# Normalised values, joint value products and a two-term spread in a pipelined four-stage attention kernel

## The chip, the cores and the metric

One core of one Trainium2 chip runs the whole program. The metric is the device time of one execution in microseconds (us), the median of three runs. TensorE (PE in the rows) multiplies, VectorE (DVE), ScalarE (ACT) and GpSimd (POOL) do the elementwise work, SyncE (SP) issues the transfers.

## The reference

Sixty-four images, 256 channels of 14 x 14, go through four blocks in turn:

```python
x = _L0_conv_ref(x, ...)  # batchnorm, depthwise 3x3 + 1x1 for q, k, v; k and v resized to 7x7; 4 heads, softmax; depthwise + 1x1, MLP
x = _L1_conv_ref(x, ...)  # group norm (8 groups); linear attention: softmax(k) over channels, softmax(q) over tokens
x = _L2_conv_ref(x, ...)  # group norm (32 groups); 8-head softmax attention over 196 tokens; projection; residual
x = _L3_conv_ref(x, ...)  # group norm (32 groups); single-head attention over 196 tokens; projection; residual
```

Each group norm is `(x - mean) * rsqrt(var + eps)`, then a weight and a bias for each channel. Everything is float32.

## The kernel before

Two images (a pair) are one unit of work: 32 pairs, 392 columns each, channels in two chunks of 128 partitions. The four blocks are cut into named steps (`q0_0`, `kv1`, `gn3`, `sc2`, `t3_1` and so on). The program is a software pipeline: each engine has a table from step to a place (`PE_AT`, `ACT_AT`, `DVE_AT`, `POOL_AT`, `SP_AT`). A place divided by `SLOTS` = 128 gives the lag, by how many turns of the loop the step comes after its pair entered; the remainder gives its place in the turn. So an engine's order in one turn is that of the remainders, over steps of up to six different pairs. A place is no time: engines work in order and wait for semaphores alone. `BANK_USES` says which PSUM bank (a, b, c, e; `ps_s` has four of its own) holds the result of a TensorE step; a bank must be read out before the next step of the turn writes it.

Names that follow in the text, in the order in which a pair meets them:
- `k0`, `v0`: keys and values of block 0 from the resized convolution output `yr`, which GpSimd makes (`resize0`, `resize1`). `pw`, `mlp`: its last products.
- `stats1..3` on VectorE, `gn1..3` on TensorE (a product with a group matrix) and on VectorE (a copy out of PSUM), then `gn1..3` on GpSimd: `normalized` makes scale and shift of each channel in 20 small instructions of 128x4 (a square root by Newton steps), and then applies them with four instructions of 128x196 (`xn`). `high` (ScalarE, to float32r) and `low` (VectorE, the rest) split the normalised values in two terms for products in float32r. These feed `kv0..3`, `q1` (block 1), `hq`, `hk`, `hv` (block 2), `v3_0..3`, `q3` (block 3).
- `keys0..3`: the exponentials of block 1's keys times the reciprocal of their sum, on GpSimd. `ctx`, `out`: the products behind them.
- `sc0..3` scores of block 2 (four heads at a time), `max` on VectorE, exponentials `sc` on ScalarE, `tn` transposes and their copies, `av` products. `rden`, `rt`: reciprocals of the sums, turned. `rep0`, `rep1`: the reciprocals spread over the channels by a product with the 0/1 matrix `heads`, `proj` behind them.
- `s3`, `probs3_0`, `probs3_1` (probabilities of block 3 times the reciprocal, on GpSimd), `t3`, `o3`.

Of the kernel before, what the change touches and what calls it, by code (L numbers as in the profile page):

```python
# [22 lines left out]
R7 = 7  # L23
# [15 lines left out]
    "x": -128, "res": 204, "hop": 486, "hop_out": 665, "store": 691,  # L39
# [38 lines left out]
}  # L78

POOL_AT = {  # L80
    "resize0": 64, "resize1": 73, "probs0": 146, "probs1": 164, "gn1": 301, "keys0": 347, "keys1": 356, "keys2": 365,
    "keys3": 374, "gn2": 393, "gn3": 640, "rows3": 667, "probs3_0": 694, "probs3_1": 722,
}

# [37 lines left out]
def build(nc, a):  # L122
    ctx = ExitStack()
    with ctx:
# [399 lines left out]
        def _(pool):  # L524
# [7 lines left out]
            def alone():  # L532

                pool.sem_inc(pool_held, 1)
# [1013 lines left out]
```

## Time and profile before

| | |
|---|---|
| median of 3 runs | 2321.23 us (2320.8 to 2322.84) |
| the profiled execution | 2331.84 us, its span 2329.6 us |
| mean granted TensorE clock | 0.975 |
| PE busy | 2158.8 us (93%) |
| DVE busy | 1851.9 us (79%) |
| ACT busy | 1443.0 us (62%) |
| POOL busy | 1493.3 us (64%) |

Busy times are unions over an engine's instructions in the one profiled execution. Times of "start to start" in the text are differences of the start column of a timeline, and take in the pipelining that durations do not show.

### The profile page before, as it was taken

The page shows a single profiled execution, that of the slowest core. Times are in us where ns is not written, and L with a number is a line of the kernel's source. Part 1 is how long each engine was busy: PE and PEld are TensorE (multiplying, and loading weights), DVE is VectorE, ACT ScalarE, POOL GpSimd, SP SyncE. Part 2 cuts the span into 40 slices and gives each one's busy share as a digit, 9 for nine tenths or more (in the row PEclk, how much of TensorE's full clock was granted, in tenths as well). Part 3 has the DMA queues.
Part 4 walks back from the last instruction along what each step waited for, and adds up shares of the span by engine and source line. Part 5 has one row for each costly group of instructions (what it writes and reads, how often), then busy time and mean ns, then how long its engine had stood idle before and what let it go on. Part 6 is the DMA issues. An engine that isn't in the chain of part 4 may idle for free. (4 is left out here: it accounts for less than half of the span.)

```text
span 2329.6 us, 59692 instructions
## 1 busy us (share of the span) xinstructions
PE 2158.8 (93%) x15488; PEld 1724.9 (74%) x15488; DVE 1851.9 (79%) x4359; ACT 1443.0 (62%) x4819; POOL 1493.3 (64%) x3274
## 2 busy tenths in 40 slices
PE   5679999999999999999999999999999999999987
PEld 4456777777777777778777777777777777777775
DVE  6678788888888888888888888888888888887542
ACT  2246666666666666666666676666667666666663
POOL 3665667676666767666676766667676666775422
PEclk8699999999999999999999999999999999999997
DMA  3000011000000000000000001000000001000000
GB/s 117 14 22 22 15 36 36 34 21 14 34 34 34 34 34 21 14 34 34 34 34 27 28 14 34 34 34 34 21 34 14 34 34 34 28 29 29 15 29 21
DMA packets 29829, 70.24 MB, mean 30 GB/s; under 512 B 6260, under 2 KB 7104, under 8 KB 29760
## 3 DMA queue, kind: packets, MB, share of 16 engines
q1 hardware_dynamic: 26928, 67.68, 8.3%
q10 hardware_dynamic: 2832, 1.73, 0.3%
q8 instruction: 33, 0.54, 0.1%
q14 instruction: 36, 0.29, 0.0%
HBM read 30.86 MB, written 12.85 MB: 19 GB/s over the span
## 5 line engine op out<-in xcount | busy, mean ns | idle before, releaser
L831 ACT ACTIVATE e<-ps_s,nm 98x196 f32<-98x196 f32 x1024 | 421.5, 431 | 80.6 <-DVE nm L955 80.6
L1159 DVE SCALAR_TENSOR_TENSOR y<-opad,w_dw,y 128x406 f32<-128x406 f32 x512 | 303.9, 646 | 0.0
L1140 DVE SCALAR_TENSOR_TENSOR y<-xpad,w_dw,y 128x406 f32<-128x406 f32 x512 | 297.9, 644 | 0.0
L955 DVE TENSOR_REDUCE nm<-ps_s 98x4 f32<-98x784 f32 x256 | 244.7, 969 | 54.8 <-PE ps_s L1167 52.3
L590 POOL TENSOR_SCALAR xn<-x,gn_scale,gn_shift 128x196 f32<-128x196 f32 x384 | 264.5, 701 | 21.3 <-POOL gn_shift L585 21.3
L568 POOL TENSOR_TENSOR gn_t<-gn_group 128x4 f32<-128x4 f32 x96 | 29.6, 308 | 325.6 <-DVE gn_group L1005 249.6
L838 ACT COPY pt<-ps_s 98x392 f32<-98x392 f32 x512 | 223.4, 508 | 13.5 <-PE ps_s L1217 13.4
L1093 DVE TENSOR_TENSOR xs<-xn,xs 128x392 fp32r<-128x392 f32 x192 | 133.0, 695 | 108.9 <-ACT xs L788 106.8
L831 ACT ACTIVATION_READ_ACCUMULATOR e<-ps_s,nm 98x1 f32 x1024 | 217.1, 212 | 0.0
L1217 PE MATMUL ps_s<-w_eye,e 98*98 98x98 f32 x2048 | 202.6, 252 | 2.9 <-ACT e L831 2.7
L1217 PEld LDWEIGHTS ps_s<-w_eye,e 98*98 98x98 f32 x2048 | 187.2, 131 | 8.8 <-ACT e L831 4.8
L1167 PE MATMUL ps_c<-ws_v,xs 128*98 128x256 f32 (+1 forms) x960 | 139.1, 292 | 36.6 <-DVE xs L1093 36.6
L788 ACT CAST xs<-xn 128x392 fp32r<-128x392 f32 x192 | 100.1, 525 | 94.7 <-POOL xn L590 88.9
L1167 PEld LDWEIGHTS ps_c<-ws_v,xs 128*98 128x98 f32 x960 | 118.4, 165 | 46.2 <-DVE xs L1093 26.5
L581 POOL TENSOR_SCALAR gn_t<-gn_t 128x4 f32<-128x4 f32 x288 | 115.9, 403 | 56.2 <-POOL gn_t L579 56.2
L611 POOL TENSOR_SCALAR kv<-kv,rk 98x256 f32<-98x256 f32 x128 | 129.2, 1016 | 31.6 <-DVE rk L1023 31.1
L845 ACT COPY a<-ps_s 128x196 f32<-128x196 f32 x128 | 41.7, 326 | 163.7 <-PE ps_s L1167 163.7
L634 POOL TENSOR_SCALAR e<-e,r 98x196 f32<-98x196 f32 x128 | 105.7, 837 | 37.1 <-DVE r L1113 29.6
L755 ACT ACTIVATE kv<-kv,nmk 98x256 f32<-98x256 f32 x128 | 64.7, 507 | 100.4 <-DVE nmk L1017 100.3
L1167 PE MATMUL ps_s<-k,q 32*98 32x196 f32 x2048 | 118.8, 345 | 2.7 <-ACT k L807 1.4
L579 POOL TENSOR_TENSOR gn_t<-gn_t,gn_half 128x4 f32<-128x4 f32 x288 | 104.9, 364 | 22.6
L936 DVE BATCH_NORM_STATS2 gn_stats<-x 128x6 f32<-128x196 f32 x384 | 110.9, 351 | 9.2 <-DVE x L1049 5.3
(235 smaller groups left out, 5820.0 us busy)
## 6 DMA issues: line engine op xcount, KB each, us to landing
x_in<-in_x SPq DMA_DIRECT2D x32, 392.0 KB, 3.1
x_res<-in_x SPq DMA_DIRECT2D x32, 392.0 KB, 3.2
x2b<-x SPq DMA_DIRECT2D x32, 392.0 KB, 3.3
out<-x SPq DMA_DIRECT2D x32, 392.0 KB, 3.3
out_pairs<-out SPq DMA_DIRECT2D x32, 392.0 KB, 2.4
w_q<-in_q SPq DMA_DIRECT2D x3, 256.0 KB
w_k<-in_k SPq DMA_DIRECT2D x3, 256.0 KB
w_v<-in_v SPq DMA_DIRECT2D x3, 256.0 KB
```

The lines of the kernel that those rows point to most:

```text
L581: link(g.tensor_scalar(t.t[:], t.t[:], 1.5, None, ALU.add))
L590: g.tensor_scalar(dst[:, c, of_image(i)], src[:, c, of_image(i)], t.scale[:, j:j + 1], t.shift[:, j:j + 1], ALU.mult, ALU.add).then_inc(t. ...
L611: g.tensor_scalar(kv[:, j, 0:CH], kv[:, j, 0:CH], rk[:, j:j + 1], None, ALU.mult).then_inc(k_scaled.sem, 1)
L831: s.activation(e2[:, j, tc], tile(use)[0:HALF, of_image(tc)], ACT.Exp, bias=nm2[:, j, tc:tc + 1], accum_out=den2[:, 2 * i + tc, h:h + 1]). ...
L838: s.copy(turned(j), tile(use)[0:HALF, 0:N2]).then_inc(emptied(use), 1)
L936: v.bn_stats(t.stats[:, j], src[:, j // 2, of_image(j % 2)]).then_inc(t.stat_steps.sem, 1)
L955: v.tensor_reduce(out=nm2[:, two], in_=ps_s[0:HALF, two, 0:N2].rearrange("p b (c n) -> p b c n", c=2), axis=AX.X, op=ALU.max, negate=True) ...
L1093: v.tensor_tensor(dst[:, 1, c], src[:, c], dst[:, 0, c], ALU.subtract).then_inc(gn[n].low.sem, 1)
L1140: v.scalar_tensor_tensor(out=dst, in0=window(xpad, c, k, CR), scalar=tap, in1=dst, op0=ALU.mult, op1=ALU.add).then_inc(conv1_steps.sem, 1)
L1159: v.scalar_tensor_tensor(out=dst, in0=window(opad, c, k, CR), scalar=tap, in1=dst, op0=ALU.mult, op1=ALU.add).then_inc(conv2_steps.sem, 1)
L1167: return nc.tensor.matmul(dst, lhsT, rhs, start=start, stop=stop)
L1217: last = nc.tensor.transpose(tile(use)[0:HALF, of_tile(sc, tc)], e2[:, j, tc, sc * HALF:(sc + 1) * HALF], eye[0:HALF, 0:HALF])
```

## The change

1. `v0`: the two images' values come from one product over 128 columns of weights (both images side by side in `yr`), not from one product for each image over a doubled copy of `yr`. The resize on GpSimd no longer writes the doubled copy. ScalarE takes the result out in four copies instead of two.
2. `rep0`, `rep1`: the reciprocals `rt2` are kept as two float32r terms (ScalarE makes the first, VectorE the rest), `heads` as float32r, and the spread is two float32r products of 392 columns for each `rep`, not two float32 products of 196.
3. `normalized` becomes `coefficients`: GpSimd makes scale and shift alone. Applying them (`norm1..3`), the scaling of the keys (`keys0..3`) and of block 3's probabilities (`probs3_0`, `probs3_1`) go to ScalarE.
4. All five tables and `BANK_USES` are made anew (one line of them stands below).

```diff
 POOL_AT = {
-    "resize0": 64, "resize1": 73, "probs0": 146, "probs1": 164, "gn1": 301, "keys0": 347, "keys1": 356, "keys2": 365,
-    "keys3": 374, "gn2": 393, "gn3": 640, "rows3": 667, "probs3_0": 694, "probs3_1": 722,
+    "resize0": 128, "resize1": 144, "probs0": 208, "probs1": 240, "gn1": 352, "gn2": 432, "gn3": 672, "rows3": 704,
...
-                link(g.tensor_copy(yr[:, c, :, 1, 0:T7], yr[:, c, :, 0, 0:T7]))
...
-                for c in range(KC):
-                    for i in range(2):
-                        j = 2 * c + i
-                        alone()
-                        g.tensor_scalar(dst[:, c, of_image(i)], src[:, c, of_image(i)], t.scale[:, j:j + 1],
-                                        t.shift[:, j:j + 1], ALU.mult, ALU.add).then_inc(t.done.sem, 1)
...
+                        p = pair_of(t, u, ACT_AT[f"keys{j}"])
+                        if p is not None:
+                            act.wait_ge(k_rsum.sem, k_rsum.at(p, j + 1))
+                            s.activation(kv[:, j, 0:CH], kv[:, j, 0:CH], ACT.Copy, scale=rk[:, j:j + 1]).then_inc(k_scaled.sem, 1)
...
+                    for n, src, dst in ((1, x1, xn1), (2, x2, xn2), (3, x3, xn3)):
+                        for c in range(KC):
+                            p = pair_of(t, u, ACT_AT[f"norm{n}_{c}"])
+                            if p is not None:
+                                act.wait_ge(gn[n].steps.sem, gn[n].steps.at(p + 1, 0))
...
+                                    s.activation(dst[:, c, of_image(i)], src[:, c, of_image(i)], ACT.Identity,
+                                                 scale=gn[n].scale[:, j:j + 1], bias=gn[n].shift[:, j:j + 1]
+                                                 ).then_inc(gn[n].done.sem, 1)
...
+                            for j in (2 * i, 2 * i + 1):
+                                s.activation(e3[:, j], e3[:, j], ACT.Copy, scale=r3[:, j:j + 1]).then_inc(p3_done.sem, 1)
...
-                        v.tensor_copy(rt2[:], tile("rt")[0:H2, 0:N2]).then_inc(emptied("rt"), 1)
+                        v.tensor_tensor(rt2[:, 1], tile("rt")[0:H2, 0:N2], rt2[:, 0], ALU.subtract).then_inc(emptied("rt"), 1)
...
-                        for i in range(2):
-                            last = product(tile("v0")[:, i * CH:(i + 1) * CH],
-                                           lambda k: yr[:, k, i].rearrange("p a n -> p (a n)"), lambda k: w["v0"][:, k])
+                        product(tile("v0")[:, 0:CH], lambda k: yr[:, k].rearrange("p i n -> p (i n)"),
+                                lambda k: w["v0"][:, k]).then_inc(filled("v0"), 1)
...
-                            for c in range(KC):
-                                last = mm(tile(use)[:, of_image(c)], w["heads"][:, c], rt2[:, of_image(i)], True, True)
+                            product(tile(use)[:, 0:N2], lambda k: heads[:, c], lambda k: rt2[:, k]).then_inc(filled(use), 1)
```

Where the instructions stand, at the three places that matter below. TensorE from `hq0` to `sc0`, before (the third row is `v0`, the fourth `gn1`):

```order
L1167 MATMUL ps_c<-xs2,ws_q2 128x392 x6
...
L1167 MATMUL ps_b<-xs2,ws_k2 128x392 x6
...
L1167 MATMUL ps_e<-w_v0,yr 128x256 x4
...
L1167 MATMUL ps_a<-gn1_mine,w_group32 128x8
...
L1167 MATMUL ps_s<-k2,q2 98x196 x8
```

and after:

```order
L1173 MATMUL ps_c<-xs2,ws_q2 128x392 x6
...
L1173 MATMUL ps_a<-xs2,ws_k2 128x392 x6
...
L1173 MATMUL ps_b<-gn1_mine,w_group32 128x8
...
L1173 MATMUL ps_c<-w_v0,yr 128x256 x2
...
L1173 MATMUL ps_s<-k2,q2 98x196 x8
```

`v0` has two products instead of four and has moved behind `gn1`; a `rep` row reads `ps_b<-rt2,w_heads 128x196 x2` before and `ps_c<-rt2,heads 128x392 x2` after, four products a pair in both, in float32r after.

ScalarE at the end of a turn, from the second `ctx` copy to the split of block 3's input, before (`xs3` is the `high` step, `q0` and `pt2` copies out of PSUM, `e2` the exponentials of `sc2`):

```order
L778 ACTIVATE cx<-ps_c,rq 128x256 x2
...
L831 ACTIVATE e2,den2<-ps_s,nm2 98x196 x2
...
L788 CAST xs3<-xn3 128x392
...
L701 COPY q0<-ps_e 128x392
...
L788 CAST xs3<-xn3 128x392
L831 ACTIVATE e2,den2<-ps_s,nm2 98x196 x2
...
L831 ACTIVATE e2,den2<-ps_s,nm2 98x196 x4
```

and after:

```order
L758 ACTIVATE cx<-ps_e,rq 128x256 x2
...
L834 ACTIVATE e2,den2<-ps_s,nm2 98x196 x6
...
L774 ACTIVATE xn3<-x3,gn3_shift,gn3_scale 128x196 x2
...
L676 COPY q0<-ps_c 128x392
L774 ACTIVATE xn3<-x3,gn3_shift,gn3_scale 128x196 x2
L841 COPY pt2<-ps_s 98x392
...
L785 CAST xs3<-xn3 128x392
```

The turn ends there; the next one begins with three more `COPY pt2` and then the second `CAST xs3`. Two pairs of normalisations now stand ahead of the casts, and the exponentials of `sc2` ahead of both.

ScalarE around block 2's split, before (`qt3` is the `q3` copy, `s0` an exponential of block 0):

```order
L838 COPY pt2<-ps_s 98x392
...
L788 CAST xs2<-xn2 128x392
...
L788 CAST xs2<-xn2 128x392
...
L862 ACTIVATE qt3<-ps_c,qu3 128x392
L725 ACTIVATE s0<-s0 98x392
```

and after:

```order
L857 COPY v3t<-ps_c 98x257
L841 COPY pt2<-ps_s 98x392
...
L774 ACTIVATE xn2<-x2,gn2_shift,gn2_scale 128x196 x4
...
L785 CAST xs2<-xn2 128x392
...
L785 CAST xs2<-xn2 128x392
...
L841 COPY pt2<-ps_s 98x392 x3
```

The four normalising instructions stand straight ahead of the two casts, and three `pt2` copies have moved behind them.

## Rows read from the trace of the kernel before

**Rows 1.** Windows: length, then busy us of PE, PEld, DVE, ACT, POOL, clock, DMA.

```profile
1201.00:1269.06 68.06, 65.60 (x484) 52.59 (x482) 57.81 (x136) 44.78 (x150) 46.96 (x103) 1.00 0.08 29
267.50:2106.70 1839.20, 1772.05 (x13012) 1420.34 (x13011) 1553.69 (x3640) 1207.79 (x4048) 1271.20 (x2757) 1.00 0.08 29
```

**Rows 2.** Waits of TensorE, 267.5 to 2106.7: total us, times, longest.

```profile
PE ps_b L1459 <- POOL e L634: 35.8, 27, 1.4
PE ps_c L1167 <- DVE xs L1093: 21.8, 26, 1.2
PE ps_b L1167 <- DVE xs L1093: 9.0, 27, 0.5
```

**Rows 3.** Timeline of TensorE, one turn: start, us, tiles, idle before.

```profile
1201.00 1.48 PE L1167 MATMUL ps_e<-y,w_q 128*128 128x392 f32 x4
...
1205.98 0.96 PE L1167 MATMUL ps_c<-ws_v,xs 128*98 128x258 f32 x6 [0.80 <-DVE xs L1093]
1206.77 1.59 PE L1217 MATMUL ps_s<-w_eye,e 98*98 98x98 f32 x16
1208.15 0.96 PE L1167 MATMUL ps_b<-ws_v,xs 128*98 128x258 f32 x6
1208.95 1.48 PE L1167 MATMUL ps_a<-y,w_o 128*128 128x392 f32 x4
...
1211.21 0.31 PE L1167 MATMUL ps_e<-gn_mine,w_group 128*128 128x8 f32 x2
...
1212.25 1.58 PE L1167 MATMUL ps_e<-y,w_o 128*128 128x392 f32 x4
...
1224.11 0.87 PE L1167 MATMUL ps_s<-pt,v 98*32 98x196 f32 x16
1224.91 1.33 PE L1167 MATMUL ps_c<-xs,ws_q 128*128 128x392 f32 x6
1226.09 1.23 PE L1167 MATMUL ps_b<-xs,ws_k 128*128 128x392 f32 x6
1227.16 1.89 PE L1167 MATMUL ps_e<-w_v,yr 128*128 128x256 f32 x8
1228.88 0.28 PE L1167 MATMUL ps_a<-gn_mine,w_group 128*128 128x8 f32 x2
...
1234.18 0.93 PE L1167 MATMUL ps_b<-rt,w_heads 8*128 8x196 f32 x4
1235.04 0.56 PE L1295 MATMUL ps_a<-w_eye,p 98*128 98x98 f32 x4
```

**Rows 4.** Timeline of GpSimd: first and last coefficient instruction, block 2, block 3.

```profile
1211.97 0.39 POOL L568 TENSOR_TENSOR gn_t<-gn_group 128x4 f32<-128x4 f32 x1 [7.20 <-DVE gn_group L1005]
...
1220.47 0.20 POOL L585 TENSOR_TENSOR gn_shift<-w_gn_b,gn_t 128x4 f32<-128x4 f32 x1
...
1259.82 0.38 POOL L568 TENSOR_TENSOR gn_t<-gn_group 128x4 f32<-128x4 f32 x1
...
1267.76 2.89 POOL L585 TENSOR_TENSOR gn_shift<-w_gn_b,gn_t 128x4 f32<-128x4 f32 x1
```

**Rows 5.** Groups by shape, whole span: busy us, mean ns | idle before.

```profile
L831 ACT ACTIVATE e<-ps_s,nm 98x196 f32<-98x196 f32 x1024 | 421.5, 431 | 80.6 <-DVE nm L955 80.6
L748 ACT ACTIVATE act<-x,bn_shift,bn_scale 128x392 f32<-128x392 f32 x64 | 45.7, 714 | 13.0 <-DVE x L986 11.9
L778 ACT ACTIVATE cx<-ps_c,rq 128x256 f32<-128x256 f32 x64 | 26.9, 471 | 57.2 <-PE ps_c L1167 57.2
L788 ACT CAST xs<-xn 128x392 fp32r<-128x392 f32 x192 | 100.1, 525 | 94.7 <-POOL xn L590 88.9 <-PE ps_a L1402 3.4
L1093 DVE TENSOR_TENSOR xs<-xn,xs 128x392 fp32r<-128x392 f32 x192 | 133.0, 695 | 108.9 <-ACT xs L788 106.8
```

**Rows 6.** Timeline of ScalarE: an exponential and the next of its kind.

```profile
1249.28 0.43 ACT L831 ACTIVATE e<-ps_s,nm 98x196 f32<-98x196 f32 x1
...
1249.68 0.43 ACT L831 ACTIVATE e<-ps_s,nm 98x196 f32<-98x196 f32 x1
```

More of the change, by code:

```diff
@@ L457, in build @@
         FOLDED = KC * 4
-        EARLY_STEPS = PLAIN + FOLDED + 6
+        EARLY_STEPS = PLAIN + FOLDED + 7
         @block.sync
@@ L604, in step @@
                                             ALU.mult).then_inc(l0_probs.sem, 1)
-                    for j in range(4):
-                        p = pair_of(t, u, POOL_AT[f"keys{j}"])
-                        if p is not None:
-                            pool.wait_ge(k_rsum.sem, k_rsum.at(p, j + 1))
-                            alone()
-                            g.tensor_scalar(kv[:, j, 0:CH], kv[:, j, 0:CH], rk[:, j:j + 1], None, ALU.mult).then_inc(k_scaled.sem, 1)
                     p = pair_of(t, u, POOL_AT["rows3"])
@@ L676, in split_weights @@
                     s.copy(high, src).then_inc(early_high, 1)
+                s.copy(heads[:], w["heads"][:]).then_inc(early_steps, 1)
                 act.wait_ge(early_steps, EARLY_STEPS)
@@ L716, in step @@
                             act.wait_ge(*full(p - 1, latest("o0_0", "o0_1")))
-                        src = tile("v0")[:].rearrange("p (i m d) -> p i m d", i=2, m=2)
-                        for hl in range(2):
-                            half = slice(64 * hl, 64 * hl + 64)
-                            s.copy(v0[half, :, :, half], src[half, :, :, half]).then_inc(emptied("v0"), 1)
+                        src = tile("v0")[:, 0:CH].rearrange("p (m d) -> p m d", m=2)
+                        for i in range(2):
+                            for hl in range(2):
+                                half = slice(64 * hl, 64 * hl + 64)
+                                s.copy(v0[half, i, :, half], src[64 * i:64 * i + 64, :, half]).then_inc(emptied("v0"), 1)
                     for i in range(2):
@@ L779, in step @@
                                              scale=rq[:, c, i:i + 1]).then_inc(emptied(use), 1)
+                    for n, src, dst in ((1, x1, xn1), (2, x2, xn2), (3, x3, xn3)):
[3 more added lines that the diff above has]
+                                act.wait_ge(gn[n].steps.sem, gn[n].steps.at(p + 1, 0))
+                                if n == 1 and has_before(p):
+                                    act.wait_ge(*read(p - 1, f"out{c}"))
+                                if n == 2:
+                                    act.wait_ge(gn[2].low.sem, gn[2].low.at(p, 0))
+                                if n == 3 and has_before(p):
+                                    act.wait_ge(*full(p - 1, latest("s3_0", "s3_1")))
+                                for i in range(2):
+                                    j = 2 * c + i
+                                    s.activation(dst[:, c, of_image(i)], src[:, c, of_image(i)], ACT.Identity,
+                                                 scale=gn[n].scale[:, j:j + 1], bias=gn[n].shift[:, j:j + 1]
+                                                 ).then_inc(gn[n].done.sem, 1)
                     for n, src, dst, readers in splits:
@@ L817, in step @@
                             s.copy(v2[:, i].rearrange("p c n -> p (c n)"), tile(use)[0:HALF, :]).then_inc(emptied(use), 1)
+                    p = pair_of(t, u, ACT_AT["rt"])
+                    if p is not None:
+                        act.wait_ge(*full(p, "rt"))
+                        if has_before(p) and not comes_after("rt", latest("rep0", "rep1")):
+                            act.wait_ge(*full(p - 1, latest("rep0", "rep1")))
+                        s.copy(rt2[:, 0], tile("rt")[0:H2, 0:N2]).then_inc(rt_high.sem, 1)
                     for g in range(GROUPS):
@@ L843, in step @@
                             if has_before(p):
-                                act.wait_ge(*read(p - 1, f"rep{i}"))
+                                act.wait_ge(*read(p - 1, f"rep{g % 2}"))
                             s.copy(a2[:, i, g % 2], tile(use)[:, 0:TOK]).then_inc(emptied(use), 1)
@@ L1060, in step @@
                     if p is not None:
-                        dve.wait_ge(*full(p, "rt"))
-                        if has_before(p) and not comes_after("rt", latest("rep0", "rep1")):
-                            dve.wait_ge(*full(p - 1, latest("rep0", "rep1")))
-                        v.tensor_copy(rt2[:], tile("rt")[0:H2, 0:N2]).then_inc(emptied("rt"), 1)
-                    for i in range(2):
-                        use = f"rep{i}"
+                        dve.wait_ge(rt_high.sem, rt_high.at(p, 1))
+                        v.tensor_tensor(rt2[:, 1], tile("rt")[0:H2, 0:N2], rt2[:, 0], ALU.subtract).then_inc(emptied("rt"), 1)
+                    for c in range(KC):
+                        use = f"rep{c}"
                         p = pair_of(t, u, DVE_AT[use])
@@ L1404, in step @@
                         last.then_inc(filled("rt"), 1)
-                    for i in range(2):
-                        use = f"rep{i}"
+                    for c in range(KC):
+                        use = f"rep{c}"
                         p = pair_of(t, u, PE_AT[use])
```

67 lines of the change are left out of this document (28 added, 39 removed), and 60 rows, old and new, of tables (ACT_AT, DVE_AT, PE_AT).

## The prediction

> **What bounds the kernel now.** I read the windows first. In one turn of the loop (the work of one pair on every engine) TensorE is busy 65.60 of 68.06 us, VectorE 57.8, GpSimd 47.0, ScalarE 44.8, at a granted clock of 1.00, the higher of its two levels (2.4 GHz) [rows 1]. So TensorE is the bound. The stretch from 267.5 to 2106.7 holds 27 turns of 1839.2 / 27 = 68.1 us; the rest of the span is filling and draining. Next I read TensorE's waits in that stretch. There are three, each once a turn [rows 2]: before the transposes `t3_1`, for the probabilities from GpSimd, 35.8 / 27 = 1.3 us; before `v3_1`, for the split of block 3's input, 0.8; before `kv0`, for block 1's, 0.3. Together 2.5 us, and 65.6 + 2.5 = 68.1: the turn is explained. All three end on a chain through GpSimd: the first names it, and the other two are group norms whose coefficients and normalisation it makes. Then I read the timelines of TensorE and GpSimd around these waits.
>
> **The change part by part.**
> *Values of block 0.* `v0` takes 1228.88 - 1227.16 = 1.72 us start to start for eight instructions (each float32 product is two) [rows 3]. Half of the products go, the width of each is the same: -0.86 us a turn.
> *The spread.* A `rep` takes 1235.04 - 1234.18 = 0.86 us for four instructions [rows 3]. It becomes two float32r products of 392 columns. The nearest row is `hq0`, six float32r products of 392 columns in 1226.09 - 1224.91 = 1.18 us, 0.197 each [rows 3]: 0.39 instead of 0.86, twice, -0.94 us. Bounds: nothing saved (0.86 stays, if eight rows of weights cost more than I think), or 0.94. I take 0.94, since the column count is what the other rows follow. TensorE's work falls to 65.6 - 0.86 - 0.94 = 63.8 us.
> *The three waits.* The probabilities, keys and normalisations leave GpSimd. `t3_1` now waits for two ScalarE instructions that stand some 8 us of TensorE work ahead of it in the new order, so the 1.3 us goes. The other two chains keep the coefficients on GpSimd, and the question is what is late next.
> *ScalarE's new work.* An application of scale and bias to 128x196 is not in the trace. Below it lies the exponential of 196 columns, 0.43 us long and 0.40 from start to start, read-out of its sum included [rows 5, 6]; above it the relu of twice the columns with both operands, 0.71 [rows 5]. I take 0.46 a step: it has the relu's operands and the exponential's length. Twelve make 5.5 us. Keys and probabilities: eight, by the `ctx` copy with a scale, 0.47 long, 0.42 a step [rows 5]: 3.4. Two more copies for `v0` and one for `rt`: 0.9. ScalarE goes from 44.8 to 54.6 us of some 65, VectorE stays at 57.8 (its `rt` changes from a copy to a subtraction of the same 392 columns), GpSimd drops well below both. None is the bound by its sum; the order must decide.
> *Block 3's chain, at the turn's end.* In the new order ScalarE has, between the end of the second `ctx` product and `v3_1`: the `ctx` copies 0.84, six exponentials 2.4, four normalisations 1.84, and seven copies or casts of 392 columns (0.525 long, 0.43 a step [rows 5]) 3.0, together 8.1. Then `low` on VectorE, 0.6 to 0.7 [rows 5], and handing over, some 0.4: 9.1. TensorE does in that time `q0_1`, both `out`, `tn2`, `k0`, `pw0`, `gn2` and `av2`, all of which stand before between 1201.00 and 1212.25 [rows 3], with two `v3` products (0.79 and 0.80) and the wait of 0.8 among them: 11.25 - 0.79 - 0.80 - 0.81 = 8.85. The wait left is 0.3 us, from 0 to 1.3 (if a normalisation takes 0.71).
> *Block 2's chain.* From `gn2` to `hq0` the trace has 1224.91 - 1211.21 = 13.7 us without a wait [rows 3]; the new order puts `v3_1` and `v3_0` in and takes one `av` (1224.91 - 1224.11 = 0.80) out: 14.5 us of cover. The chain: 0.76 to the first coefficient instruction, 8.7 for twenty of them (1211.97 to 1220.67) [rows 3, 4], four normalisations 1.84, two casts 0.86, `low` 0.65, handing over 0.5: 13.3. Spare 1.2 us. But block 3's twenty took 1259.82 to 1270.65, 10.8 us, with one of them at 2.89 instead of 0.20 [rows 4]; at that pace block 2's chain is 15.4, and `hq0` waits 0.9.
> *Block 1's chain* has 34.5 - 16.6 = 17.9 us of TensorE work over it in the new order, by the same laying end to end, against 13.3 to 15.4: no wait.
> *Transfers.* The five on SP's queue have moved in the turn. No engine's wait in the stretch names one [rows 2], and each is asked for more than 5 us before its reader: nothing.
> I take 1.0 us of waits a turn: 0.3, half of 0.9, and 0.3 for banks read out late by a fuller ScalarE. The turn is 64.8 us, 3.3 less. Over 27 turns -89, and -1 in the draining turns. Against the profiled span: 2329.6 - 90 = 2239.6. The profiled execution is 2.2 us longer than its span, and 10.6 longer than the median, so the median falls to 2321.2 - 90 = 2231.
>
> **The rivals.**
> *A, no wait is left.* The turn is TensorE's 63.8: 27 x 4.3 = 116, 2205 us. For it: GpSimd, the source of all three waits, is nearly idle. Against: the 9.1 over 8.85 above.
> *B, the coefficients, or ScalarE behind them, are the new wait.* The small GpSimd instructions do not always take 0.20 us: 2.89 beside VectorE's depthwise taps [rows 4]. If block 2's and block 3's chains both lose about one us more than I took, waits are 2 to 2.5 us a turn: 27 x 2.3 = 62 to 27 x 1.8 = 49 less, 2259 to 2272. Against: in block 2's place the same instructions took 8.7.
> The Trainium skill, "GPSIMD Engine Reference", section Key points, says that GpSimd shares its SBUF interfaces with VectorE and is held up by VectorE instructions with two SBUF inputs; the depthwise taps are such, and the 2.89 us row agrees. By that rule the chains stay slow wherever the taps stand beside them, which is B.
> *C, slower: ScalarE in its order becomes the bound.* Elementwise work that waited on its own engine now stands in ScalarE's queue, and every TensorE bank is read out behind it. The turn passes 68.1 us when TensorE waits over 4.3 us. At 0.71 a normalisation the two chains gain 1.0 each and waits come to 3 at most. At 1.2 us each chain gains 3.0, the waits are 7, the turn 70.8: 2394. It decides from about 0.9 us an instruction; the rows stop at 0.71.
> The Trainium skill, "ScalarE: Activation LUTs", Rules for kernel authors, sends plain adds and multiplications to VectorE instead of ScalarE, which speaks for C; the same page's figures for an instruction with two per-partition operands give an estimate near 0.44 us a step, which speaks against it. No run here shows either yet.
> *D, nothing gained:* the float32r spread costs what it did, and the new order brings back 2.5 us of waits with some more in filling: 2300 to 2321.
>
> **How the numbers follow.** My forecast, 2215 to 2248, has 0.60; A 0.12; B 0.20; C 0.04; D 0.04. A measurement of this kernel tells 0.2% (5 us) from no change. Faster is all but C and part of D, 0.94; same 0.02; slower 0.04. The range takes in A's end and B's: 2203 to 2272.
>
> **What would show it.** In the profile after: `v0` four instructions in about 0.86 us, each `rep` two in 0.4; no wait of TensorE on GpSimd; normalisations 0.5 to 0.6 us long; TensorE at 98% or more of a turn; its largest waits before `v3_1` or `hq0`, for VectorE's `low`. The prediction is wrong if ScalarE's normalisations are far longer, if GpSimd's coefficients take over 11 us, or if TensorE waits at steps that I did not lay out, such as those held by a bank.

## The result, and the profile after

The changed kernel takes 2195.69 us (median of 4 runs, 2190.08 to 2196.51) where the kernel before takes 2321.88 beside it (4 runs): ratio 0.9452, 95% interval 0.9435 to 0.9468. It is faster, and by more than the forecast of 2231 us said: the time lies 7 us below the range's lower end, 2203.

| | before | after |
|---|---|---|
| profiled execution, its span | 2331.84, 2329.6 us | 2195.19, 2193.4 us |
| turn, mean of 27 | 68.12 us | 63.62 us |
| from the start to the second `rden` on VectorE (filling) | 267.5 us | 255.7 us |
| behind the 27 turns (draining) | 222.9 us | 220.1 us |
| PE, DVE, ACT, POOL busy, share of the span | 93, 79, 62, 64% | 96, 83, 77, 40% |

The turn is taken from one `rden` to the next here. The windows of the kernel after, one turn and 27 turns (columns as in [rows 1], to which they answer):

```profile
1204.38:1268.00 63.62, 63.53 (x476) 51.70 (x475) 56.98 (x136) 52.44 (x174) 27.34 (x81) 1.00 0.09 32
255.70:1973.30 1717.60, 1715.35 (x12800) 1396.06 (x12799) 1534.07 (x3640) 1414.50 (x4671) 739.16 (x2161) 1.00 0.09 32
```

TensorE is busy 63.53 of 63.62 us. Its list of waits from 255.7 to 1973.3, where [rows 2] had three, is empty; the list leaves out idle gaps under 0.1 us. ScalarE went from 44.8 to 52.4 us a turn, GpSimd from 47.0 to 27.3. Against the forecast for the profiled span, 2239.6, 46 us are missing: 27 x (64.8 - 63.62) = 32 in the turns, 12 in the filling, 2 in the draining.

TensorE in one turn after (compare [rows 3]; third column ahead of the tiles: the modelled length; a step's cost is the difference of two starts):

```profile
1199.24 0.28 PE L1173 MATMUL ps_e<-gn_mine,w_group 128*128 128x8 f32 x2
1199.45 0.88 PE L1173 MATMUL ps_s<-pt,v 98*32 98x196 f32 x16
1200.41 0.96 PE L1173 MATMUL ps_e<-ws_v,xs 128*98 128x258 f32 x6
...
1213.62 1.23 PE L1173 MATMUL ps_c<-xs,ws_q 128*128 128x392 f32 x6
1214.78 0.87 PE L1173 MATMUL ps_s<-pt,v 98*32 98x196 f32 x16
...
1216.89 1.11 PE L1173 MATMUL ps_c<-w_v,yr 128*128 128x256 f32 x4
1217.93 0.92 PE L1173 MATMUL ps_s<-k,q 32*98 32x196 f32 x16
...
1225.81 0.62 PE L1173 MATMUL ps_c<-rt,heads 8*128 8x392 f32 x2
1226.36 1.34 PE L1173 MATMUL ps_b<-xs,ws_k 128*128 128x392 f32 x6
```

`v0` takes 1217.93 - 1216.89 = 1.04 us, a `rep` 1226.36 - 1225.81 = 0.55. `hq0` (1213.62) doesn't wait. `v3_1` (1200.41) does, by an amount below the list's 0.1: `av2` ahead of it takes 0.96 us to the next start, where every other `av` of 16 products takes 0.80 (1224.91 - 1224.11 in [rows 3]), so 0.15 us of each turn is waiting. The elementwise work ahead of the two, on ScalarE and VectorE:

```profile
1191.88 0.84 ACT L758 ACTIVATE cx<-ps_e,rq 128x256 f32<-128x256 f32 x2
...
1199.07 0.59 ACT L785 CAST xs<-xn 128x392 fp32r<-128x392 f32 x1
...
1209.17 1.88 ACT L774 ACTIVATE xn<-x,gn_shift,gn_scale 128x196 f32<-128x196 f32 x4 [0.44 <-POOL gn_shift L587]
```

```profile
1199.66 0.17 DVE L1013 COPY gn_group<-ps_e 128x8 f32<-128x8 f32 x1 [0.74 <-PE ps_e L1173]
1199.79 0.57 DVE L1099 TENSOR_TENSOR xs<-xn,xs 128x392 fp32r<-128x392 f32 x1
...
1211.78 0.57 DVE L1000 TENSOR_TENSOR x<-ps_c,x 128x392 f32<-128x392 f32 x1 [0.74 <-PE ps_c L1173]
1212.27 1.03 DVE L1099 TENSOR_TENSOR xs<-xn,xs 128x392 fp32r<-128x392 f32 x2
```

and block 2's coefficients on GpSimd, the first, the longest and the last of twenty (compare [rows 4]):

```profile
1199.98 0.43 POOL L570 TENSOR_TENSOR gn_t<-gn_group 128x4 f32<-128x4 f32 x1 [12.00 <-DVE gn_group L1013]
...
1204.05 2.01 POOL L581 TENSOR_TENSOR gn_t<-gn_t,gn_half 128x4 f32<-128x4 f32 x1
...
1208.86 0.20 POOL L587 TENSOR_TENSOR gn_shift<-w_gn_b,gn_t 128x4 f32<-128x4 f32 x1
```

Block 3's chain: its `low` ends at 1199.79 + 0.57 = 1200.36, 0.05 ahead of `v3_1`, so it is what `v3_1` waits for. But ScalarE does not set that end. The cast is done at 1199.66; `low` stands in VectorE's order behind the copy of `gn2`, which waits 0.74 for TensorE's own `gn2` product (1199.24). In the kernel of 2188 us further down, whose normalisations are on GpSimd, the second cast ends 0.65 us earlier, counted from the `ctx` product, and `v3_1` comes 8.56 us behind that product as it does here. Its rows, cast, copy and `low`:

```profile
1194.59 0.55 ACT L809 CAST xs<-xn 128x392 fp32r<-128x392 f32 x1
```

```profile
1195.79 0.17 DVE L1032 COPY gn_group<-ps_e 128x8 f32<-128x8 f32 x1 [0.75 <-PE ps_e L1192]
1195.92 0.57 DVE L1118 TENSOR_TENSOR xs<-xn,xs 128x392 fp32r<-128x392 f32 x1
```

In the kernel after, `low` begins 0.13 us behind its cast, where one that only waits for its cast begins 0.03 behind: the slack of ScalarE's part is 0.1.

Block 2's `low` ends at 1213.30, 0.32 ahead of `hq0`; that `low` stands in VectorE's order behind the addition for `mlp1`, which itself waited 0.74 for TensorE, so the chain can be later than the 0.32 tells. Four normalisations take 1.88 us.

The question for the experiments: where the gain of 4.5 us a turn comes from (products, moved work, timetable), and why next to no wait is left.

### The profile page after: what moved, and what is told of

Read it like the earlier page. It is cut to its first block, busy times and chain, and to the rows that moved or that the text cites. A ratio compares the mean times of both kernels' runs of the same rounds, so it can differ in the third digit from the quotient of the medians.

```text
span 2193.4 us, 58372 instructions
## 1 busy us (share of the span) xinstructions
PE 2096.0 (96%) x15232; PEld 1692.7 (77%) x15232; DVE 1830.2 (83%) x4359; ACT 1689.1 (77%) x5556; POOL 887.0 (40%) x2570
## 4 chain that ended last, share of the span: by engine, by line
PE 88%; POOL 3%; DVE 3%; ACT 3%; issue 2%; SPq 1%; DMA 0%; DVEq 0%; POOLq 0%; ACTq 0%
PE ps_b L1173 18%; PE ps_c L1173 18%; PE ps_a L1173 17%; PE ps_e L1173 16%; PE ps_s L1173 9%; PE ps_s L1223 7%; DVE xs L1099 1%; POOL gn_y L584 1%; ACT e L834 1%; ACT xn L774 1%; PE ps_b L1461 1%; PE ps_e L1406 0%; SPq L477 0%; PE ps_b L1299 0%; PE ps_c L1461 0%
## 5 line engine op out<-in xcount | busy, mean ns | idle before, releaser
L774 ACT ACTIVATE xn<-x,gn_shift,gn_scale 128x196 f32<-128x196 f32 x384 | 190.1, 566 | 36.1 <-POOL gn_shift L587 36.1
L1223 PEld LDWEIGHTS ps_s<-w_eye,e 98*98 98x98 f32 x2048 | 186.1, 128 | 29.7 <-ACT e L834 10.8
L1099 DVE TENSOR_TENSOR xs<-xn,xs 128x392 fp32r<-128x392 f32 x192 | 107.3, 586 | 43.7 <-ACT xs L785 43.6
L598 POOL TENSOR_TENSOR p<-s,r 98x392 f32<-98x392 f32 x64 | 56.4, 882 | 194.4 <-DVE r L986 194.4
L581 POOL TENSOR_TENSOR gn_t<-gn_t,gn_half 128x4 f32<-128x4 f32 x288 | 125.9, 437 | 22.5
L1173 PE MATMUL ps_a<-xs,ws_q 128*128 128x392 f32 x576 | 126.7, 355 | 0.0
L1173 PE MATMUL ps_s<-pt,v 98*32 98x196 f32 x2048 | 114.5, 342 | 1.4 <-ACT pt L841 1.3
L1173 PEld LDWEIGHTS ps_s<-k,q 32*98 32x98 f32 x2048 | 76.5, 160 | 38.5 <-issue 29.7
L1173 PE MATMUL ps_c<-y,w_q 128*128 128x392 f32 x256 | 101.0, 518 | 4.0 <-ACT q L676 3.1
L1173 PEld LDWEIGHTS ps_a<-xs,ws_q 128*128 128x128 f32 x576 | 98.2, 189 | 0.1
L549 POOL TENSOR_TENSOR rs_d<-y 128x168 f32<-128x168 f32 x64 | 39.6, 619 | 144.2 <-DVE y L1146 139.6
```

The costliest lines, as they stand in the source:

```text
L581: link(g.tensor_tensor(t.t[:], t.t[:], t.half[:], ALU.mult))
L774: s.activation(dst[:, c, of_image(i)], src[:, c, of_image(i)], ACT.Identity, scale=gn[n].scale[:, j:j + 1], bias=gn[n].shift[:, j:j + 1]). ...
L1099: v.tensor_tensor(dst[:, 1, c], src[:, c], dst[:, 0, c], ALU.subtract).then_inc(gn[n].low.sem, 1)
L1173: return nc.tensor.matmul(dst, lhsT, rhs, start=start, stop=stop)
L1223: last = nc.tensor.transpose(tile(use)[0:HALF, of_tile(sc, tc)], e2[:, j, tc, sc * HALF:(sc + 1) * HALF], eye[0:HALF, 0:HALF])
```

## Experiments

Times are medians; three rounds beside the kernel before unless "one run" is said. "Work" and "waits" are means over some 20 turns of TensorE's start-to-start times and of its idle gaps over 0.1 us; a shorter gap counts as work. Differences between kernels of different rounds carry up to 7 us of uncertainty: the kernel before had medians from 2321.9 to 2328.6 beside them.

**The two savings on TensorE.** Taken back in the kernel after:

```diff
-                        product(tile("v0")[:, 0:CH], ...).then_inc(filled("v0"), 1)
+                        for i in range(2):
+                            last = product(tile("v0")[:, i * CH:(i + 1) * CH], ...)
...
-                            product(tile(use)[:, 0:N2], lambda k: heads[:, c], lambda k: rt2[:, k]).then_inc(filled(use), 1)
+                            for i in range(2):
+                                last = mm(tile(use)[:, of_image(i)], heads[:, c], rt2[:, 0, of_image(i)], True, True)
```

> The kernel after, with TensorE's two savings taken back and all else kept: the values' product is done twice (the second copy isn't read), and the spread is two float32 products of 196 columns from the first term of the reciprocals, which is then no longer split to float32r (the second term is made and not used). Theory (after the change TensorE alone sets the turn, so work counts in full): the turn goes from 63.6 to 63.6 + 0.69 for v0 + 0.68 for the two rep = 65.0 us, the time to 2196 + 27 x 1.37 + 2 for the draining = 2235 us, no waits on TensorE. Rival (the chains through GpSimd and ScalarE are as long as TensorE's work, so that more work is partly hidden): under 64.5 us a turn, below 2222.

2239.68 us, ratio 0.9646 (0.963 to 0.9663), turn 65.06, no wait. `v0` takes 1.90 instead of 1.04, each `rep` 0.86 instead of 0.55: 1.48 us a turn, and the turn grew by 1.44. The theory holds: with no wait left, TensorE's work counts in full.

The same two savings alone, in the kernel before, with ScalarE's new copy `rt` at place 541 and, in a second kernel, at 547:

```diff
 ACT_AT = {
+    "rt": 541,
```

> The kernel before with its own timetable and GpSimd's elementwise work, and only the two savings on TensorE: joint values and the two-term spread (the copy of the reciprocals to ScalarE, the rest on VectorE). Theory (work and waits add): TensorE's work falls by 1.3 to 1.4 us a turn and the three waits of 2.5 stay, the turn is 66.7, the time 2321 - 38 = 2283. Rival (the savings shorten what covers the chain of block 3's probabilities and of block 1's norm, so the waits grow by as much): waits of 3 to 3.9 us, turn 67.3 to 68.1, 2300 to 2321.

2387.28 us, ratio 1.0286 (1.0261 to 1.031): slower, with less work. Neither theory had this. The copy stood ahead of two copies of block 2's transposes for which `av3` waits; it waits for TensorE's `rt` first:

```profile
1248.33 0.87 PE L1192 MATMUL ps_s<-pt,v 98*32 98x196 f32 x16 [1.16 <-ACT pt L865]
1250.34 2.33 PE L1192 MATMUL ps_c<-xs,ws_q 128*128 128x392 f32 x6 [1.14 <-DVE xs L1118]
```

The `hq0` behind two waits reads 2.33 us where it takes 1.33 in [rows 3]; the granted clock while it runs is 0.50.

> The kernel before with the two savings on TensorE again, but ScalarE's copy of the turned reciprocals now stands behind its copies of the block 2 transposes, not ahead of them (where it held up the product av3 by 1.2 us a turn in the run before this one). Theory (that place was all that was wrong): work 64.4 a turn, waits 2.4 to 3 as in the kernel before, turn 67 to 67.5, 2290 to 2305. Rival (less work in TensorE's order lets the three chains through GpSimd stand out by as much as was saved, and TensorE's clock falls behind a wait): turn 68 or more, no faster than the kernel before.

2306.94, ratio 0.9924 (0.9907 to 0.994): one copy, six places later, is worth 80 us. Turn 67.43, work 64.7, waits 2.75 (65.7 and 2.43 before). Work fell by 1.0 and waits grew by 0.3, so some of each is true: in before's timetable the savings bring 17 us (the kernel before took 2323.98 beside it), in after's 44.

**The work moved from GpSimd to ScalarE.** After's timetable, with all three pieces back on GpSimd; first in after's order of GpSimd (not before's, as the expectation says), where block 0's second probabilities stand behind the first norm:

> The kernel after with its timetable for every other engine, but normalisations, keys and block 3's probabilities back on GpSimd (in the order that GpSimd had before; the places of its table shifted together). Theory (the offload took the waits away): a normalisation takes 0.70 on GpSimd and 0.45 on ScalarE, so block 2's chain is 1.0 longer with 0.3 of slack, and the probabilities and keys wait behind GpSimd's other work: waits of 1.5 to 3 us come back, the turn is 65 to 66.6, the time 2235 to 2280. Rival (the timetable took them away, and who does the elementwise work matters little): the turn stays within 63.6 to 64.3, 2196 to 2215.

2402.82, ratio 1.0343 (1.0325 to 1.036). The largest wait is that order's doing, so this run says little of the offload:

```profile
PE ps_b L1321 <- POOL p L609: 59.4, 19, 3.1
```

Then with GpSimd's own table of the kernel before (here and in the four runs that follow):

```diff
 POOL_AT = {
-    "resize0": 128, "resize1": 144, "probs0": 208, "probs1": 240, "gn1": 352, "gn2": 432, "gn3": 672, "rows3": 704,
+    "resize0": 64, "resize1": 73, "probs0": 146, "probs1": 164, "gn1": 301, "keys0": 347, "keys1": 356, "keys2": 365,
+    "keys3": 374, "gn2": 393, "gn3": 640, "rows3": 667, "probs3_0": 694, "probs3_1": 722,
```

> After's timetable on all other engines, with normalisations, keys and block 3's probabilities on GpSimd and GpSimd's own table of the kernel before, in which block 0's second probabilities stand ahead of the first norm (in the run before this one they stood behind it and cost 3.1 us a turn). Theory (the moved work does the most): the waits on the probabilities and on the norms' chains come back with 1.5 to 3 us a turn, 2236 to 2280 and more if TensorE's clock falls behind them. Rival (the timetable does the most): a turn under 64.5, below 2220.

2233.99, ratio 0.9622 (0.9595 to 0.9648), turn 64.72, between the theory and the rival. None of before's three waits is back. The one there is stands before `av2`; ScalarE waits in its order for block 3's normalised values, and three copies for `av2` stand behind:

```profile
1220.69 0.52 ACT L811 CAST xs<-xn 128x392 fp32r<-128x392 f32 x1 [1.76 <-POOL xn L596]
1221.12 1.25 ACT L867 COPY pt<-ps_s 98x392 f32<-98x392 f32 x3
```

```profile
1222.50 0.87 PE L1194 MATMUL ps_s<-pt,v 98*32 98x196 f32 x16 [1.06 <-ACT pt L867]
```

So after's timetable takes all three waits away without the moved work. Which piece is worth the remaining 38 us:

> The kernel after with only the normalisations back on GpSimd (with before's order of GpSimd); keys and block 3's probabilities stay on ScalarE. With all three back the time was 2234 and the one wait of TensorE (0.93 us a turn, before av2) stood behind ScalarE, which waited 1.8 us in its order for block 3's normalised values. Theory (the normalisations of block 3 are that wait): 0.9 us a turn again, 2225 to 2238. Rival (keys and probabilities delayed GpSimd, so that the norm came late): no wait or under 0.3, 2196 to 2206.

2194.21, ratio 0.9431 (0.9415 to 0.9447), turn 63.61: nothing. The theory falls.

> The kernel after with only block 3's probabilities on GpSimd (before's order of GpSimd); norms and keys on ScalarE. Theory (the keys are what matters): no wait, 2190 to 2200. Rival (the wait before t3_1, 1.3 us a turn in the kernel before, comes back at a part of its size): 2205 to 2236.

2193.18, ratio 0.9451 (0.9422 to 0.9481), turn 63.62: nothing either, as the theory said.

> The kernel after with only the scaling of the keys on GpSimd (before's order of GpSimd); norms and block 3's probabilities on ScalarE. All three on GpSimd gave 2234, the norms alone 2194: so keys, probabilities, or both with the norms, make the difference. Theory (the four keys, 1 us each and straight ahead of block 3's coefficients in GpSimd's order, make the norm late, and ScalarE waits for it in its order with the copies for av2 behind): a wait before av2 of 0.5 to 1 us a turn, 2212 to 2236. Rival (it takes all three to fill GpSimd): no wait, 2190 to 2200.

2298.19, ratio 0.9885 (0.986 to 0.9911), turn 66.78, more than the theory said. GpSimd, VectorE, ScalarE and TensorE around it:

```profile
1237.71 3.90 POOL L607 TENSOR_SCALAR kv<-kv,rk 98x256 f32<-98x256 f32 x4 [6.14 <-DVE rk L1034]
1241.59 0.38 POOL L571 TENSOR_TENSOR gn_t<-gn_group 128x4 f32<-128x4 f32 x1
...
1245.96 5.16 POOL L582 TENSOR_TENSOR gn_t<-gn_t,gn_half 128x4 f32<-128x4 f32 x1
```

```profile
1246.57 4.49 DVE L1168 SCALAR_TENSOR_TENSOR y<-opad,w_dw,y 128x406 f32<-128x406 f32 x8
```

```profile
1254.02 0.99 ACT L777 ACTIVATE xn<-x,gn_shift,gn_scale 128x196 f32<-128x196 f32 x2 [2.49 <-POOL gn_shift L588]
1254.91 0.46 ACT L683 COPY q<-ps_c 128x392 f32<-128x392 f32 x1
```

```profile
1255.51 1.57 PE L1176 MATMUL ps_c<-yr,w_k 128*128 128x98 f32 x8 [1.97 <-ACT q L683]
1256.87 2.79 PE L1176 MATMUL ps_b<-y,w_o 128*128 128x392 f32 x4
1259.49 0.29 PE L1176 MATMUL ps_e<-gn_mine,w_group 128*128 128x8 f32 x2
```

The keys (3.9 us) push block 3's coefficients under eight of VectorE's depthwise taps. One coefficient instruction, 0.20 us elsewhere, begins at 1245.96 and ends at 1251.12, as the taps end (1251.06). ScalarE waits 2.49 for the result, the copy of `q0` stands behind, and `k0` waits 1.97 for that bank. In the other turns of this kernel `w_o`, behind `k0`, takes either 2.0 to 2.7 us, as here, or its usual 1.34; the end of this text comes back to that. This is the mechanism of rival B, and the page named there (the Trainium skill, "GPSIMD Engine Reference", Key points: GpSimd is held up by VectorE instructions with two SBUF inputs) agrees: the taps are such.

With all three on GpSimd the same 5.16 us stands there and costs less (2234). The traces suggest why, but no run separates it: block 3's normalisation is then not in ScalarE's order, where it holds up the copy of `q0`; only the cast stands there, further back.

> After's timetable and products with the scaling of the keys alone on ScalarE; all normalisations and block 3's probabilities on GpSimd in before's order of it. Theory (of the three moves, only the keys' matters, since they alone stand ahead of block 3's coefficients and push these beside VectorE's depthwise taps): no wait, turn 63.6, 2190 to 2200. Rival (norms and probabilities together fill GpSimd enough to make block 2's or block 3's norm late): a wait of 0.3 us or more, over 2204.

2188.02, ratio 0.942 (0.9397 to 0.9443), turn 63.62, no wait. The keys' move is the one that matters; this kernel, with less moved, is at least as fast as the kernel after (its interval overlaps). In it the taps hold up block 3's normalisations instead (6.88 us for four, 1.96 where no tap stands beside them), and nothing waits for these.

**The timetable.** Before's timetable with everything else of the change, the moved steps put right ahead of those that need them, the copy `rt` at 541 and then at 547:

```diff
 ACT_AT = {
+    "rt": 541, "norm1_0": 327, "norm1_1": 328, "norm2_0": 417, "norm2_1": 418, "norm3_0": 626, "norm3_1": 627,
+    "keys0": 349, "keys1": 354, "keys2": 357, "keys3": 358, "probs3_0": 713, "probs3_1": 718,
```

> The counterpart: before's timetable on all engines, with all other parts of the change (new products, and the normalisations, keys and probabilities on ScalarE, put in right ahead of the instructions that need them). Theory (offload and work make the gain, and the timetable the rest): no waits on GpSimd, TensorE's work 65.7 - 1.4 = 64.3 and 0 to 0.8 of waits behind a fuller ScalarE; turn 64.3 to 65.1, time 2216 to 2240. Rival (without the new order ScalarE reads banks out late and the chains wait): 2 us of waits or more, over 66.3, 2270 and up. In either case what is left to the kernel after is the order's: I put it at 0.7 us of work a turn from fewer changes between float32 and float32r products, and 12 us in the filling.

2542.89, ratio 1.0951 (1.0931 to 1.0971), turn 75.02, granted clock over the turns 0.93. The theory, faster by 80 us and more, missed; the rival has the side, not the size. 2.0 us a turn of it are the wait of the copy `rt` again.

> Before's timetable with everything else of the change, the copy of the turned reciprocals now behind the transposes' copies on ScalarE. The same products alone gave 2307 with this timetable; the same moved work gave 2196 against 2234 with after's. Theory (on ScalarE the moved work stands ahead of read-outs of banks and copies that before's order has right before TensorE's products, so new waits come and TensorE's clock falls behind them): slower than the kernel before, 2350 to 2450. Rival (the place of the copy was all that was wrong in the first try): waits under 2.5 us a turn, 2230 to 2300.

2429.43, ratio 1.0423 (1.0404 to 1.0442), turn 71.65. Waits of TensorE from 500 to 1800 (18 turns; total, times, longest):

```profile
PE ps_c L1173 <- DVE xs L1099: 45.1, 36, 1.3
PE ps_c L1173 <- ACT v L814: 27.7, 19, 1.5
PE ps_b L1173 <- DVE xs L1099: 9.3, 19, 0.5
PE ps_a L1173 <- DVE gn_mine L951: 9.2, 18, 0.5
PE ps_s L1173 <- ACT a L848: 2.4, 6, 0.5
```

The theory holds: in before's order, at these places, the moved work costs some 120 us over the products alone (2306.94); in after's it gains 38. Other places for it in before's order were not tried. The wait for GpSimd before `t3_1` is gone, but those before `v3_1` and `kv0` stand there, at 1.3 and 0.5 us instead of 0.8 and 0.3, and new ones before `rep1` (for its bank) and `hq0`. A part of the loss is clock: 0.97 granted over the turns.

The timetable alone: the kernel of 2233.99 us with the old products as in the first run.

> After's timetable on all engines but GpSimd, which keeps its table and its elementwise work of the kernel before, and TensorE's old products (values' product twice, spread of 196 float32 columns from the first term). So the timetable by itself. Theory (timetable and products add here, because TensorE's order has cover to spare): 64.7 + 1.44 = 66.2 us a turn, 2274, of 2322: the timetable gives about 48 us alone. Rival (a longer turn gives GpSimd time, and the wait before av2 goes): 65.1, 2240.

2284.99, ratio 0.9839 (0.9816 to 0.9861), turn 66.12, the same wait of 0.92 before `av2`. As the theory said, 1.40 a turn over its counterpart (the time is 11 us over the theory's 2274).

**How much slack the chains have.** Four, then twelve (one run), more small instructions in block 2's coefficients:

```diff
+                for _ in range(4 * (n in (2,))):
+                    link(g.tensor_tensor(t.t[:], t.y[:], t.y[:], ALU.mult))
                 link(g.tensor_tensor(t.scale[:], t.y[:], weight[:], ALU.mult))
```

> The kernel after with four more small instructions (their result is overwritten) in the coefficients of block 2's norm on GpSimd, some 1.4 us in the chain from gn2 to hq0, which has 0.3 us of slack. Theory (a chain's delay beyond its slack is paid once, one for one): a wait of 1.1 us before hq0, turn 64.7, time 2196 + 30 = 2226. Rival (a wait of this size takes TensorE's clock down with it, as before's timetable with the moved work showed, where the product behind a wait of 1.37 took 2.33 us instead of 1.18): 3 us a turn and more, over 2275.

2204.49, ratio 0.9486 (0.947 to 0.9502), turn 64.09. Well under the theory. The coefficients go from 9.07 to 10.46 us, 1.39 more; `hq0` comes 0.36 later, counted from `gn2`, so the slack was 1.0 and not the 0.3 that the theory read off one row. `hq0` waits 0.22, and work reads 0.25 longer though nothing was added on TensorE: 0.15 on the step ahead of the wait, 0.11 on `hq0` itself, at a granted clock of 1.00.

> The kernel after with twelve more small instructions in block 2's coefficients, not four: some 3.9 us more in the chain instead of 1.3, which gave 0.5 us a turn. Theory (a long wait takes TensorE's clock down for the products behind it): a wait of 2.8 us before hq0 and 1 to 3 us more for slower products, turn 67.5 to 70, 2300 to 2365. Rival (the wait costs itself): 64.1 + 2.6 = 66.7, 2278.

2312.54, turn 67.56. Wait 2.45, work 1.40 longer. TensorE's timeline and two windows:

```profile
1211.20 1.99 PE L1175 MATMUL ps_c<-xs,ws_q 128*128 128x392 f32 x6 [2.44 <-DVE xs L1101]
1213.12 1.54 PE L1175 MATMUL ps_s<-pt,v 98*32 98x196 f32 x16
1214.58 1.53 PE L1175 MATMUL ps_a<-xs,ws_k 128*128 128x392 f32 x6
```

```profile
1211.20:1214.58 3.38, 3.38 (x22) 2.06 (x22) 2.72 (x13) 3.06 (x8) 0.65 (x1) 0.56 0.00 0
1222.00:1260.00 38.00, 38.00 (x271) 30.68 (x270) 35.41 (x82) 30.55 (x107) 15.16 (x43) 1.00 0.11 42
```

The granted clock in the 3.4 us behind the wait is 0.56, near the lower of its two levels (1.2 GHz), and 1.00 again later in the turn. `hq0` takes 1.92 instead of 1.16, `av3` 1.46 instead of 0.80. It is not so in every turn: in 5 of 19 the clock stays at 1.00 behind the same wait, and in others it falls later. The twelve make the coefficients 3.6 us longer and `hq0` comes 2.6 later, so the slack is 1.0 by this run too, and a delay of 2.6 beyond it cost 3.9 a turn. The Trainium skill, "TensorE: Matmul & The Clock Gate", Part 1, describes such a gate; the levels agree with these rows.

More work on ScalarE ahead of block 3's normalisations (one run):

```diff
+                                for e in range(2 if (n, c) == (3, 0) else 0):
+                                    s.activation(spare[:, e], src[:, c, of_image(e)], ACT.Identity,
+                                                 scale=gn[n].scale[:, e:e + 1], bias=gn[n].shift[:, e:e + 1])
```

> The kernel after with two more applications of scale and bias (128x196, to a buffer that nobody reads) on ScalarE ahead of block 3's normalisations, 0.9 us more in the chain from the second ctx product to v3_1, which by the trace ends 0.05 us before v3_1 starts. Theory (that chain has no slack; the prediction put 9.1 us of chain over 8.85 of cover): a wait of about 0.85 before v3_1 and 0.2 of shadow, turn 64.6, 2222. Rival (TensorE has slack there that the row at the chain's end hides): turn under 63.9, below 2203.

2211.3, turn 64.40, 0.78 more for 0.9 added. The amount is nearly the theory's, the place is not: `k0` waits 0.24 for the copy of `q0` and `av2` 0.24 for copies of transposes, both behind the normalisations in ScalarE's order, and `v3_1` no more than in the kernel after. It comes 9.34 us behind the `ctx` product instead of 8.56, all of the 0.78, and `low` now begins 0.03 behind its cast. So ScalarE's order has 0.1 us of slack there, whichever reader feels the rest.

**TensorE's order by itself.** In the kernel after, these places of `PE_AT` (eight in the end, where the expectation counts ten), and `q3_0`, `q3_1`, `t3_1` on ScalarE to fit:

```diff
-"t0_0": 172, "q3_0": 657, "q3_1": 667, "hk0": 416, "av3": 543, "q1_1": 352, "t3_1": 733, "rep1": 574
+"t0_0": 175, "q3_0": 667, "q3_1": 666, "hk0": 414, "av3": 545, "q1_1": 348, "t3_1": 734, "rep1": 571
```

> The kernel after with ten steps moved by a place or two in TensorE's order (and three on ScalarE), so that float32r products stand together: TensorE goes between float32 and float32r 16 times a turn, not 26 (34 in the kernel before). Theory (each such change costs some 0.09 us: the order alone took 0.73 us of work off the turn with eight fewer): work 62.7 a turn, and if no wait comes, 2196 - 25 = 2171. Rival (the change between the types costs nothing; what the order saved lies in which product stands behind which): work within 0.2 us of 63.6, 2190 to 2201, or slower if a moved step waits for its bank.

2197.78, ratio 0.9458 (0.9443 to 0.9474), work 63.59, no wait listed. Ten changes of type fewer brought 0.03 us. The theory falls.

Before's order without its chains; in the kernel before, with products that read weights in place of the normalised inputs and of the probabilities, so that its results are not the reference's:

```diff
-                            split_product(tile(use)[0:HALF, :], lambda a, k: xs1[:, a, k, of_tile(j // 2, j % 2)],
+                            split_product(tile(use)[0:HALF, :], lambda a, k: ws["q1"][:, a, k, 0:HALF],
...
-                                                               e3[:, 2 * i + tc, sc * HALF:(sc + 1) * HALF],
+                                                               w["p2"][0:HALF, 0, sc * HALF:(sc + 1) * HALF],
```

> The kernel before, but the products v3, q3 and kv and the transposes t3 read weights in place of the normalised inputs and probabilities (block 3's and the keys' and values' results are therefore not the reference's); their waits on these chains go, the order and the shapes of all instructions stay. It asks what before's order costs TensorE when it doesn't wait. Theory (part of what I read as a dearer order is the shadow of the waits: the steps beside a wait read 0.1 to 0.2 us longer): work falls from 65.7 to 65.0 or less, turn the same. Rival (the order itself is dearer): work stays at 65.5 to 65.8 with no idle time.

2318.99 (one run; the kernel before took 2328.56 beside it), turn 68.38: the three waits are gone and another stands in their place, 1.95 us a turn before block 2's transposes `tn2`, for ScalarE's exponentials. Work as a whole reads 66.3, so the sum didn't fall as the theory said; step by step it did beside the removed waits: `out0`, ahead of `v3_1`, reads 1.19 instead of 1.47, `kv3` ahead of `t3_1` 1.44 instead of 1.60, `rep1` ahead of `kv0` 0.86 instead of 0.93, together 0.51. The steps from the new wait on read longer, the granted clock over the turns being 0.99. A wait has a shadow on the step ahead of it: the profile counts idle time from that step's modelled end, while an unhindered next step starts ahead of that end, by 0.30, 0.16 and 0.07 us behind these three steps. Removing before's three chains alone makes the turn no shorter.

| us (turn) | before's timetable | after's timetable |
|---|---|---|
| as it was | 2321.88 (68.12) | 2284.99 (66.12) |
| new products | 2306.94 (67.43) | 2233.99 (64.72) |
| moved work | not run | 2239.68 (65.06) |
| both | 2429.43 (71.65) | 2195.69 (63.62) |

## Why the prediction was wrong

The direction, TensorE as the bound and the end of its waits on GpSimd were right. The size was not: 2231 forecast, 2195.69 measured.

- **Work.** 63.8 forecast, 63.6 measured, from errors that cancel. `v0` saved 0.86 as worked out, for the same place in the order. The two `rep` saved 0.62, not 0.94: each takes 0.55, not 0.39. The single products' starts tell why: the four old ones of a `rep` are 0.27, 0.17, 0.17 and 0.25 apart, the two new ones 0.28 and 0.27, those inside `hq0` 0.18. The first and the last product of a `rep` each cost some 0.09 more in both kernels, and the share by six of `hq0` hid that; halving `v0` took out inner products alone (0.216 each). And the shadow of the three waits, 0.5, which the working took for work, went with them, while the 0.15 before `v3_1` now counts as work.
- **The step that failed: "I take 1.0 us of waits a turn", made of 0.3, half of 0.9, and 0.3 for banks.** Of these 0.15 us came, none over the 0.1 of the list. For block 3 the working put the chain at 9.1 over a cover of 8.85. From the end of the second `ctx` product (about 1191.85) the second cast took to 1199.66, 7.8 us, not 8.1; with `low` (0.57, not 0.6 to 0.7) and the handing over seen here (0.03 and 0.05, not 0.4) the chain is 8.5, counted from 1191.85. The cover, from the start of `q0_1` (1191.68) to where `v3_1` could have started, was 8.6: the 8.85 had the 0.28 of shadow ahead of `v3_1` in it. So chain and cover meet within 0.1, as the slack found above says. What `v3_1` does wait for, the copy of `gn2` ahead of `low` in VectorE's order, the working didn't have. For block 2 it charged half of 0.9, by coefficients of 10.8 us; they took 9.1, and the spare 1.2 us of the working is nearly the 1.0 that both delays found. No bank was late, though ScalarE's order has no room left: 0.9 us more there cost 0.78.
- **ScalarE.** 0.46 a normalisation was right: it measures 0.45 a step. The estimate from the figures of the Trainium skill, "ScalarE: Activation LUTs", section What ACT_TABLE_LOAD costs, was 0.44, and this trace agrees. The 54.6 us a turn were 52.4. Rival C's price of 0.71 or more didn't occur. The moved work does make a kernel slower, but through its place in the order and TensorE's clock, at 0.45 us an instruction: 2429 with before's timetable. That is rival C's outcome in another order, by another mechanism than its price.
- **Rival A** (no wait left, 2205, chance 0.12) is what happened but for the 0.15 us; its 2205 is 9 us high: 5 by the turns, 3 by the draining and 12 by the filling, less 11 by the offset below.
- **Rival B** is real in this kernel and was avoided by the keys' move: with the keys on GpSimd the coefficients meet the taps and one takes 5.16 us.
- **Filling and median.** The working had 0 for the filling, and it fell by 12 in the profiled runs. Kernels with the same turn of 63.6 reached the second `rden` between 250.8 and 255.7, and one kernel's executions differ by 6 us, so much of this is the execution, not the change. The forecast also kept before's profiled-to-median offset of 10.6; after's is -0.5. That took 11 of the 46 missing microseconds off again.
- **What caused the waits before.** The reading that all three were GpSimd's load was wrong. With the load back on GpSimd and after's timetable, none of the three returned (64.72 a turn); with the load gone and before's timetable only the one before `t3_1` went. The other two were a matter of what stood over each chain. Which of the five tables did it no run separates.

What stays open: a quarter of a microsecond of the 4.5 a turn (2.42 waits, 0.51 shadow, 0.86 and 0.62, less 0.15, make 4.26), and how the filling's 12 us split between change and execution.

## What to carry to other kernels

In a software pipeline with one order per engine, price a moved instruction by what stands behind it in the new engine's queue, not by its length: the same moves gained 38 us in one order and lost some 120 in the other, and one copy six places later was worth 80. Count the slack of each chain before charging for it, on every engine that it passes (here a copy on VectorE, not ScalarE's part, released `v3_1`), keep the sign open when chain and cover differ by less than the error of their terms, and give "no wait left" the chance that this implies. Look first for the smallest part of an offload that matters: here four instructions a turn out of twenty.

## What the hardware showed that was not expected

- TensorE's clock can fall behind short waits, in some turns and not in others. Behind 1.97 us of waiting (the keys on GpSimd) `w_o` took 2.62 us in one turn and 1.34 in another; the same stretch in both:

```profile
1255.51:1259.49 3.98, 3.98 (x12) 2.76 (x13) 0.57 (x1) 3.98 (x10) 0.00 (x0) 0.57 0.00 0
1322.64:1326.62 3.98, 3.67 (x32) 2.58 (x33) 1.31 (x4) 3.98 (x10) 0.66 (x3) 1.00 0.00 0
```

  The turns between 500 and 1800 us whose granted clock fell below 1.00 in the 4 us behind the wait: 14 of 19 behind 2.44 us (twelve instructions more), 10 of 15 behind 1.97 and none of 5 behind 1.58 (keys on GpSimd), 1 of 19 behind 1.35 (the kernel before), none of 20 behind 0.66 to 1.06 (all on GpSimd), 8 of 19 behind 1.5 (before's order without its chains), and 10 of 18 behind two waits of 1.16 and 1.14 with one step of products between them. In these runs a wait cost itself, a shadow of 0.1 to 0.3 us ahead, about 0.1 behind, and, in the mean of all turns, 1.3 us (2.44) or 0.8 us (1.97 and 1.58) of slower work as well.
- A GpSimd instruction of 4 columns took 5.16 us beside a run of eight depthwise taps on VectorE (4.49 us), and ended 0.06 us behind them; beside two taps one took 2.01.
- Changing between float32 and float32r products cost TensorE nothing that this reordering could measure: ten changes fewer in a turn, 0.03 us.
